# Deformable convolution and covariance attention on one core: square root as a recurrence on S = Z Y, and a shorter prologue

## The chip, the cores and the metric

One core of a Trainium2 chip. The time is the device time of one execution in microseconds, the median of several. The engines are called PE (matrix products), DVE (vector), ACT (activation), POOL (general), and SP (which here only issues transfers). All data are float32.

## The reference

The input x is 8 images of 64 channels, 24 x 24 pixels. Two residual blocks follow each other:

```
n  = groupnorm(x, 32 groups)
off = conv3x3(pad(n), w_off)                 # 128 output channels: y and x offsets of each of 64 channels
xd = bilinear sample of pad(n) at grid + off # per channel
x1 = x + w_pw @ relu(batchnorm(xd) * gamma + beta)

m  = groupnorm(x1, 32 groups)
A  = covariance of the 64 channels of m      # one 64 x 64 matrix per image
Y, Z = A / trace(A), I
for i in range(5):                           # Newton-Schulz iterations
    T = 0.5 * (3 I - Z @ Y)
    Y, Z = Y @ T, T @ Z                      # (Z is not needed after the last)
v  = mean over rows of Y * sqrt(trace(A))
a  = sigmoid(w2 @ relu(w1 @ v + b1) + b2)
out = x1 + a * m
```

## The kernel before

The work is written out by hand, one instruction stream per engine, with semaphores between them (a queue of an engine never reorders). Images are held in pairs, two images of 64 channels on 128 partitions, so there are four tiles of x (T = 4).

Prologue. SP issues the four tiles of x (lines 309 and 311), then waits until DVE has zeroed the buffer of w_pw (line 770) and issues six small transfers (lines 315 to 320); behind these in SP's queue stands, for each image from 1 on, the copy of its map shifted by a row (line 342), which the convolution of that image needs (line 584). ACT issues the two transfers of w_off. DVE first makes constants with 48 memsets, two 32x32 transposes and four comparisons for the identity (line 763; with it PE can start) and four operations for the matrix pairm that averages a pair of channels (line 767). Then come statistics of the first tile (line 799), a product with pairm on PE (line 562), a square root on ACT, and two ACT fills of the map of image 0, the second of them the copy shifted by a row (lines 430 and 432). PE meanwhile runs four fillers, products of the identity with itself whose result nobody reads (stay_busy, line 555), and turns w_off into nine taps by products with the identity (line 572, 24 instructions; a float32 product is two instructions), then eight fillers more (line 579). DVE copies four of six columns of taps from PSUM to SBUF (line 820) and ACT two (line 469). Then PE convolves the images in order: 12 instructions at line 588 with weights of row pairs, 12 at line 594 with those of the last row. In the convolution of image 0 the statistics product of the other three tiles stands between the two parts.

Middle. For each image ACT evicts the offsets and DVE does the sampling (lines 830 to 866). Then one far sample per partition is found, gathered, and put in its place; PE runs 26 and 15 fillers there (lines 621 and 625) ahead of and behind the batch norm products (lines 623 and 624). The pointwise products, group norm, transposes and covariances follow.

Recurrence. The four pairs are cut into halves of two (NS_HALF). DVE makes Y from the covariance (line 1061), Z = 1.5 I - 0.5 Y (line 1065) and 1.5 Y. PE forms Y Y; DVE turns that into the next Y (line 1074). Three times: PE forms Z Y (64 columns a product, line 695), DVE the factor T = 1.5 I - 0.5 Z Y, PE T [Y, Z] (128 columns), and DVE (line 1084, half 0) and ACT (line 534, half 1) copy 256 columns each back. One filler stands behind each group of products. At the end, row sums (line 1089), two rounds of matrix times vector (line 703) with DVE steps between give the vector of the last product; then scaling (line 1098), the two small layers (lines 738 and 741), and the result (lines 545 and 1109), which SP stores.

Of the kernel before, what the change touches and what calls it, by code (L numbers as in the profile page):

```python
# [5 lines left out]
def deform_conv_then_covariance_attention(nc, x, w_off, gamma, beta, w_pw, w1, b1, w2, b2, out):  # L6
# [17 lines left out]
    P = 128  # L24
# [30 lines left out]
    with ctx:  # L55
# [23 lines left out]
        lane = sb("lane", [P, 2, 32])  # L79
        lanet = sb("lane_of_partition", [P, 2, 32])  # L80
        halves = sb("one_half", [P, 32])
        pairm = sb("mean_of_group_pair", [P, P])
# [67 lines left out]
        u = sb("ns_col_sum", [P, T])  # L150
        zu = sb("ns_z_u", [P, T])
# [19 lines left out]
        P_BANK, YZ_BANK = (0, 3), (1, 2)  # L171
# [28 lines left out]
        gm_ok = sem("conv_map_ready")  # L200
        shifted_in = [sem(f"map_{b}_shifted_by_a_row_in") for b in range(B)]
# [48 lines left out]
        y_ok = sem("ns_y_ready")  # L250
        p_ps = sem("ns_product_in_psum")
        t_ok = sem("ns_t_ready")
        yz_ps = sem("ns_next_y_z_in_psum")
        yz_ok = [sem(f"ns_y_z_ready_{k}") for k in range(2)]
# [42 lines left out]

        def rows(ap):
            return ap.rearrange("p (r k) -> p r k", k=W)
# [112 lines left out]
        def _(act):  # L412
# [13 lines left out]
            def fill_gmap(b):  # L426
                if b == 0:
                    act.wait_ge(maps_zero, 5)
                full, gn = normalised(b)
                last = nc.scalar.activation(interior(b, 0, 2, 2), full, **gn)  # L430
                if b == 0:
                    last = nc.scalar.activation(interior(b, C, 1, 2), full, **gn)
                last.then_inc(gm_ok, 1)
# [34 lines left out]
            act.wait_ge(wtrans, 1)  # L468
            nc.scalar.copy(wt[:, 4:6, :].rearrange("p a n -> p (a n)"), ps[:, 6, 0:2 * P]).then_inc(wready, 1)
# [16 lines left out]
            act.wait_ge(wtrans, 2)  # L486
# [45 lines left out]
            for k in range(ITERS - 2):  # L532
                act.wait_ge(yz_ps, 2 * k + 2)
                nc.scalar.copy(YZ[:, T // 2:T].rearrange("p t m c -> p (t m c)"),
                               ps[:, YZ_BANK[1], 0:T * C]).then_inc(yz_ok[1], 1)
# [13 lines left out]
        def _(pe):  # L549
# [25 lines left out]
            for at, (first, second) in enumerate(((0, 3), (1, 4), (2, 5), (6, 6), (7, 7), (8, 8))):  # L575
                tap_to(lower, 5 + at // 4, at % 4, first)
                last = tap_to(upper, 5 + at // 4, at % 4, second)
            last.then_inc(wtrans, 1)
            stay_busy(8, 7)
            def conv(b, par, between=None):  # L580

                pe.wait_ge(gm_ok, b + 1)
                if between is None:
                    pe.wait_ge(shifted_in[b], 16)
                chunks = ((0, CA, F0, slice(0, C), 0), (CA, PAIRS, BANK, slice(C, P), GR))
# [4 lines left out]
                if between is not None:  # L590
                    between()
                for kx in range(3):
# [6 lines left out]
            pe.wait_ge(wready, 2)  # L599
# [19 lines left out]
            pe.wait_ge(wready, 3)  # L619
# [70 lines left out]
            def products(t0, t1, bank, left, right, width):  # L690

                for t in range(t0, t1):
                    for par in range(2):
                        h = slice(C * par, C * par + C)
                        last = mm(ps[h, bank, width * (t - t0):width * (t - t0 + 1)], left[h, t], right[h, t],  # L695
                                  start=True, stop=True)
                return last

            def vectors(col, left, right):
                for t in range(T):  # L700
                    for par in range(2):
                        h = slice(C * par, C * par + C)
                        last = mm(pstat[h, col + t:col + t + 1], left[h, t], right[h, t:t + 1], start=True, stop=True)
                last.then_inc(vec_ps, 1)

            Y, Z = YZ[:, :, 0], YZ[:, :, 1]
            both = YZ[:].rearrange("p t m c -> p t (m c)")

            def first_products(g):
                pe.wait_ge(y_ok, g + 1)  # L710
                products(*NS_HALF[g], P_BANK[g], Y, Y, C).then_inc(p_ps, 1)
# [8 lines left out]
            for g in range(2):  # L720
                first_products(g)
            stay_busy(1, 5)
            for k in range(ITERS - 2):

                for g, (t0, t1) in enumerate(NS_HALF):
                    pe.wait_ge(yz_ok[g], k + 1)
                    products(t0, t1, P_BANK[g], Z, Y, C).then_inc(p_ps, 1)
                stay_busy(1, 5)
                for g, (t0, t1) in enumerate(NS_HALF):
                    pe.wait_ge(t_ok, 2 * k + g + 1)  # L730
                    products(t0, t1, YZ_BANK[g], Tm, both, 2 * C).then_inc(yz_ps, 1)
                stay_busy(1, 5)
            pe.wait_ge(vec_ok, 1)
            vectors(216, Z, u)
            pe.wait_ge(vec_ok, 2)
            vectors(224, Y, zu)
            pe.wait_ge(vec_ok, 3)
# [7 lines left out]
        def _(dve):  # L745
# [3 lines left out]
            for j in range(32):  # L749
                v.memset(lane[:, 0, j:j + 1], float(j))  # L750
            for j in range(16):
                last = v.memset(lane[:, 1, 2 * j:2 * j + 2], float(j))
            then(last)
            v.memset(halves[:], 0.5)
            v.memset(ident[:], 0.0)
            then(v.memset(pairm[:], 0.0))
            wait()
            for k in range(2):
                last = v.transpose(lanet[:, k], lane[:, k])
            link(last)  # L760
            for q in range(0, P, 32):
                blk = slice(q, q + 32)
                last = v.tensor_tensor(ident[blk, blk], lane[blk, 0], lanet[blk, 0], ALU.is_equal)
            last.then_inc(consts, 1)
            for q in range(0, P, 32):
                blk = slice(q, q + 32)
                last = v.scalar_tensor_tensor(pairm[blk, blk], lane[blk, 1], lanet[blk, 1, 0:1], halves[blk],
                                              ALU.is_equal, ALU.mult)
            last.then_inc(mats, 1)
            v.memset(wpn[:], 0.0).then_inc(wpn_zero, 1)  # L770
            v.memset(eps[:], EPS)
            v.memset(vv[:], 0.0)
            v.memset(zero[:], 0.0)
            v.memset(neg1[:], -1.0).then_inc(image_done, 1)
            v.memset(ones[:], 1.0)

            def over(m, k):

                g = m[:].rearrange("p (g k) -> p g k", k=k)
                return [g[:, :, j:j + 1].broadcast_to([P, P // k, k]) for j in range(k)]  # L780

# [23 lines left out]
            def gn1_scale(g, t0, t1):  # L805
# [3 lines left out]
                link(v.tensor_tensor(dev, mv1[:, t0:t1, 0], view[:, :, 0], ALU.subtract))  # L809
                link(v.tensor_tensor(dev, dev, dev, ALU.mult))  # L810
                v.tensor_tensor(v1[:, t0:t1], dev, view[:, :, 1], ALU.add).then_inc(gn1_v, 1)
                dve.wait_ge(gn1_sd, g)
                link(v.reciprocal(r1[:, t0:t1], v1[:, t0:t1]))
                v.scalar_tensor_tensor(nb1[:, t0:t1], view[:, :, 0], -1.0, r1[:, t0:t1], ALU.mult,  # L814
# [322 lines left out]
```

## Time and profile before

| | us |
|---|---|
| median of 3 runs | 129.51 |
| lowest, highest | 128.79, 130.43 |
| profiled execution, its own time | 129.9 |
| its span, first to last instruction | 128.1 |
| PE busy | 96.7 |
| DVE busy | 94.7 |
| ACT busy | 58.5 |
| mean granted clock of PE | 0.893 |

1.8 us of the profiled execution lie outside its span. Busy time of an engine is the union of its instructions; a share of busy time mixes stages that have different limits. The granted clock is a share of 2.4 GHz; 0.50 is the lower level, 1.2 GHz.

### The profile page before, as it was taken

How to read it: one execution, taken by the hardware profiler on the slowest of the kernel's cores; microseconds unless marked ns; L12 is line 12 of the kernel's file. 1: busy time of each engine (PE TensorE's matmuls, PEld its weight loads, DVE VectorE, ACT ScalarE, POOL GpSimd, SP SyncE). 2: the span in 40 equal slices, each digit the busy share in tenths (PEclk: the TensorE clock that was granted, in tenths of full speed). 3: DMA queues.
4: the chain of work that ended last, by engine and by line, in shares of the span. 5: the costliest groups of instructions: out<-in, count | busy, mean ns of one | idle time of the engine just before them, and what ended most of it. 6: DMA issues, size and time to landing. Idle time of an engine off the chain costs nothing.

```text
span 128.1 us, 1828 instructions
## 1 busy us (share of the span) xinstructions
PE 96.7 (75%) x631; PEld 75.2 (59%) x631; DVE 94.7 (74%) x296; ACT 58.5 (46%) x92; POOL 9.8 (8%) x22
## 2 busy tenths in 40 slices
PE   0699999999999999944910029999999899994100
PEld 0599777666776667713600029998697897873100
DVE  7829175859999999999999999685779846333600
ACT  3059567669697794674049000029126270120600
POOL 7003500000000003200000601000000000000000
PEclk9999999999999999998685555999999999998555
DMA  4920718753885491794000040000000000000076
GB/s 112 303 55 0 153 37 232 185 145 77 249 231 143 135 255 31 148 276 128 0 3 0 0 125 0 0 8 0 0 0 0 0 0 5 0 5 0 0 192 177
DMA packets 6393, 10.92 MB, mean 85 GB/s; under 512 B 1648, under 2 KB 3440, under 8 KB 6384
## 3 DMA queue, kind: packets, MB, share of 16 engines
q1 hardware_dynamic: 5824, 8.93, 26.1%
q0 software_dynamic: 400, 1.58, 5.3%
q10 hardware_dynamic: 160, 0.30, 0.9%
q8 instruction: 5, 0.08, 0.3%
q14 instruction: 4, 0.03, 0.1%
HBM read 3.10 MB, written 5.14 MB: 64 GB/s over the span
## 4 chain that ended last, share of the span: by engine, by line
PE 64%; DVE 17%; ACT 6%; issue 3%; DMA 3%; POOL 1%; DVEq 0%; POOLq 0%
PE ps L588 18%; PE ps L555 14%; PE ps L594 11%; PE ps L667 4%; PE ps L695 4%; DMA slot_map<-gmap_scratch,gather_rows 3%; PE ps L630 3%; PE ps L572 2%; PE ps L653 2%; DVE result L931 2%; DVE rows_at_x L851 2%; ACT rows_at_x L445 1%; PE ps L638 1%; ACT positive_offsets L460 1%; DVE result L1109 1%
## 5 line engine op out<-in xcount | busy, mean ns | idle before, releaser
L555 PE MATMUL ps<-ident 128*128 128x128 f32 x134 | 22.1, 323 | 15.3 <-DMA slot_map<-gmap_scratch,gather_rows 11.6
L555 PEld LDWEIGHTS ps<-ident 128*128 128x128 f32 x134 | 19.8, 230 | 17.0 <-issue 12.9
L588 PE MATMUL ps<-gmap,w_off_taps 128*128 128x336 f32 (+1 forms) x96 | 27.7, 437 | 0.0
L588 PEld LDWEIGHTS ps<-gmap,w_off_taps 128*128 128x128 f32 x96 | 17.5, 188 | 10.0 <-issue 3.3
L594 PE MATMUL ps<-gmap,w_off_taps 64*128 64x288 f32 (+1 forms) x96 | 15.9, 443 | 0.0
L594 PEld LDWEIGHTS ps<-gmap,w_off_taps 64*128 64x128 f32 x96 | 11.0, 185 | 3.3 <-issue 2.7
L451 ACT COPY offsets<-ps 64x576 f32<-64x576 f32 x8 | 5.0, 629 | 9.3 <-PE ps L594 9.3
L851 DVE COPY_PREDICATED rows_at_x<-positive_offsets,x_differences 128x864 f32<-128x864 int32 x8 | 9.0, 1130 | 0.0
L613 PE MATMUL ps<-x_halves,ident 128*128 128x288 f32 x16 | 6.2, 542 | 3.6 <-DMA x_halves<-in_x_dram 3.6
L858 DVE TENSOR_TENSOR rows_at_x<-rows_at_x,offsets 128x864 f32<-128x864 f32 x8 | 8.4, 1054 | 0.0
L866 DVE TENSOR_TENSOR rows_at_x<-rows_at_x,hmap 128x864 f32<-128x864 f32 x8 | 8.4, 1053 | 0.0
L430 ACT ACTIVATE gmap<-x_pairs,gn_shift,gn_rstd 64x576 f32<-64x576 f32 x8 | 7.0, 876 | 1.0 <-DVE gn_shift L814 0.9
L445 ACT COPY rows_at_x<-x_differences 128x864 f32<-128x864 f32 x8 | 7.2, 904 | 0.0
L498 ACT ACTIVATE bn_scalars<-bn_scalars,eps 128x1 f32<-128x1 f32 x1 | 0.3, 295 | 14.5 <-DVE bn_scalars L982 14.5
L613 PEld LDWEIGHTS ps<-x_halves,ident 128*128 128x128 f32 x16 | 3.9, 258 | 5.0 <-DMA x_halves<-in_x_dram 3.8
L516 ACT COPY centered_t<-ps 96x384 f32<-96x384 f32 x8 | 3.6, 475 | 5.8 <-PE ps L653 5.8
L845 DVE TENSOR_TENSOR largest_abs_offset<-abs_offsets 128x288 f32<-128x288 f32 x8 | 3.6, 455 | 3.5 <-ACT rows_at_x L445 2.1
L460 ACT ACTIVATE positive_offsets<-offsets 128x576 f32<-128x576 f32 x8 | 5.9, 740 | 0.3
L667 PE MATMUL ps<-centered_t 96*128 96x128 f32 x48 | 5.8, 278 | 0.0
L463 ACT ACTIVATE abs_offsets<-offsets 128x576 f32<-128x576 f32 x8 | 5.8, 724 | 0.0
L667 PEld LDWEIGHTS ps<-centered_t 96*128 96x128 f32 x48 | 5.5, 192 | 0.0
L994 DVE BATCH_NORM_STATS2 gn_stats<-ps 128x6 f32<-128x288 f32 x8 | 3.6, 458 | 2.3 <-PE ps L630 2.2
(183 smaller groups left out, 149.1 us busy)
## 6 DMA issues: line engine op xcount, KB each, us to landing
offset_scratch<-offsets SPq DMA_DIRECT2D x8, 288.0 KB, 2.6
gmap_scratch<-gmap SPq DMA_DIRECT2D x8, 196.0 KB, 3.1
gmap<-gmap SPq DMA_DIRECT2D x7, 189.0 KB, 2.5
hmap<-gmap SPq DMA_DIRECT2D x12, 98.0 KB, 2.5
x_pairs<-in_x_dram SPq DMA_DIRECT2D x4, 288.0 KB, 4.9
x_halves<-in_x_dram POOLq DMA_DIRECT2D x2, 576.0 KB, 7.1
out_dram<-result SPq DMA_DIRECT2D x2, 360.0 KB, 4.2
out_dram<-result SPq DMA_DIRECT2D x2, 216.0 KB, 3.0
```

What stands on the lines that cost most here:

```text
L430: last = nc.scalar.activation(interior(b, 0, 2, 2), full, **gn)
L445: nc.scalar.copy(rows3(hrow[:, par]), windows(dx[:, par, 0:HH, 0:W], 3, MC - 1)).then_inc(left_ok, 1)
L460: nc.scalar.activation(pos[:, par], kq, ACT.Relu)
L463: nc.scalar.activation(ab[:, par], kq, ACT.Abs).then_inc(abs_ok, 1)
L555: mm(ps[:, bank, 0:P], ident[:], ident[:], start=True, stop=True)
L588: mm(psf[:, par, col:col + PC * (m1 - m0)], wt[:, kx, :], conv_window(gmap[:, b], kx + 2 + 2 * GR * m0, m1 - m0), start=(kx == 0), stop=False)
L594: last = mm(psf[:, par, col:col + PC * (m1 - m0)], wt[half, 3 + kx, :], conv_window(gmap[half, b], 2 * GR - shift + kx + 2 + 2 * GR * m0, ...
L613: mm(ps[:, X1_BANK[b], 0:Q], ident[:], xh[:, b, :], start=True, stop=False)
L667: last = mm(pcov[t // (T // 2)][:, t % (T // 2)], m, m, start=(k == 0 and hh == 0), stop=(k == 2 and hh == 1))
L851: v.copy_predicated(rows3(h), windows(rows(pos[:, par, 1, :]), 3, 0).bitcast(i32), right).then_inc(along, 1)
L858: v.tensor_tensor(h, h, windows(off[:, b, :, 1], 3, 0), ALU.mult).then_inc(along, 1)
L866: v.tensor_tensor(rows3(h), rows3(h), windows(hmap[:, b, 0:HH, 1:1 + W], 3, GR), ALU.add).then_inc(along, 1)
```

## The change

Prologue: half as many lane constants; pairm is made in one operation from the identity and holds sums (the half goes into the three operations that read the products). SP waits for the first tile of x before it issues the other three. DVE instead of ACT makes the shifted copy of image 0's map. The taps are held three to a bank and evicted in two parts: the row pairs by DVE, the last row by ACT, with semaphores of their own; the convolution of image 0 waits for the pairs, and for the last row only between its two parts. The eight fillers behind the taps are gone. The constants that nobody needs yet, the zeroing of w_pw's buffer among them, move behind DVE's copy of the taps.

Recurrence: with S = Z Y and T = 1.5 I - 0.5 S the next S is S T T, so Y and Z needn't be kept. X holds per pair a vector u and the factor T, 65 columns. Each of four turns: PE forms T [u, T] (line 695's successor, bank Q), DVE (half 0) and ACT (half 1) copy 130 columns back, PE forms S T T (bank S; in the first turn with the column S u beside it, which becomes the next u by a copy of DVE), DVE makes the next T out of it, and ACT copies the next S. At the end one round of T u, and the scaling reads its result from PSUM. No fillers stand in it.

```diff
-        YZ = sb("ns_y_z", [P, T, 2, C])
-        Y15 = sb("ns_y_1_5", [P, T, C])
-        Tm = sb("ns_t", [P, T, C])
+        S = sb("ns_s", [P, T, C])
+        X = sb("ns_u_and_factor", [P, T, 1 + C])
...
             sp.dma_start(xp_[:, 0, :], x_pair[:, 0, :]).then_inc(x_in[0], 16)
+            sp.wait_ge(x_in[0], 16)
             for t in range(1, T):
...
-                    last = nc.scalar.activation(interior(b, C, 1, 2), full, **gn)
...
-            nc.scalar.copy(wt[:, 4:6, :]..., ps[:, 6, 0:2 * P]).then_inc(wready, 1)
+            act.wait_ge(wtrans, 2)
+            nc.scalar.copy(wt[:, 3:6, :]..., ps[:, 6, 0:3 * P]).then_inc(singles_ok, 1)
...
+            for k in range(ITERS - 1):
+                act.wait_ge(q_ps, 2 * k + 2)
+                nc.scalar.copy(X[:, T // 2:T], a_level(1)).then_inc(q_ok[1], 1)
+                for g, (t0, t1) in enumerate(NS_HALF):
+                    if k < ITERS - 2:
+                        act.wait_ge(t_ok, 2 * k + g + 3)
+                        if k == 0:
+                            act.wait_ge(u_ok, g + 1)
+                        nc.scalar.copy(S[:, t0:t1], b_level(g)[:, :, 1:1 + C]).then_inc(s_ok, 1)
...
-            stay_busy(8, 7)
...
-                if between is None:
+                if b:
                     pe.wait_ge(shifted_in[b], 16)
+                else:
+                    pe.wait_ge(first_shift_ok, 1)
+                    pe.wait_ge(pairs_ok, 1)
...
+            for k in range(ITERS - 1):
+                for g in range(2):
+                    pe.wait_ge(t_ok, 2 * k + g + 1)
+                    if k == 1:
+                        pe.wait_ge(u_ok, g + 1)
+                    products(g, a_level(g), factor, with_u).then_inc(q_ps, 1)
+                for g in range(2):
+                    pe.wait_ge(q_ok[g], k + 1)
+                    if k:
+                        pe.wait_ge(s_ok, 2 * k + g - 1)
+                        products(g, b_level(g)[:, :, 1:1 + C], S, square).then_inc(s_ps, 1)
+                    else:
+                        products(g, b_level(g), S, with_u).then_inc(s_ps, 1)
...
+            v.tensor_tensor(pairm[:]..., *over(ident, 2), ALU.add).then_inc(mats, 1)
...
+            v.tensor_scalar(interior(0, C, 1, 2), xp_[0:C, 0, :]..., r1[0:C, 0:1],
+                            nb1[0:C, 0:1], ALU.mult, ALU.add).then_inc(first_shift_ok, 1)
             dve.wait_ge(wtrans, 1)
-            v.tensor_copy(wt[:, 0:4, :]..., ps[:, 5, 0:4 * P]).then_inc(wready, 1)
+            v.tensor_copy(wt[:, 0:3, :]..., ps[:, 5, 0:3 * P]).then_inc(pairs_ok, 1)
+            later_constants()
             gn1_mean_var(1, T)
...
+            for k in range(ITERS - 1):
+                t0, t1 = NS_HALF[0]
+                dve.wait_ge(q_ps, 2 * k + 1)
+                v.tensor_copy(X[:, t0:t1], a_level(0)).then_inc(q_ok[0], 1)
+                for g, (t0, t1) in enumerate(NS_HALF):
+                    dve.wait_ge(s_ps, 2 * k + g + 1)
+                    v.scalar_tensor_tensor(X[:, t0:t1, 1:1 + C], b_level(g)[:, :, 1:1 + C], -0.5,
+                                           windows(id15[:], t1 - t0, 0), ALU.mult, ALU.add).then_inc(t_ok, 1)
+                    if k == 0:
+                        v.tensor_copy(X[:, t0:t1, 0], b_level(g)[:, :, 0]).then_inc(u_ok, 1)
```

## Rows read from the trace of the kernel before

**Rows 1.** Chain of waits, in order of time (start us, us, what).
```profile
5.18 0.83 DVE gn_stats L799 x2
...
6.94 2.77 PE ps L572 x24
9.71 3.01 PE ps L555 x16
12.73 3.21 PE ps L588 x12
...
17.98 3.40 PE ps L588 x12
```

**Rows 2.** Timeline, 0 to 13 us (start us, us busy, engine, operation).
```profile
1.71 0.48 DVE L752 MEMSET lane<- 128x2 f32 x16
...
2.57 0.31 DVE L759 STREAM_TRANSPOSE lane_of_partition<-lane 128x32 f32<-128x32 f32 x2
...
3.73 2.08 PE L555 MATMUL ps<-ident 128*128 128x128 f32 x8 [3.73 <-DVE ident L763]
...
5.01 0.56 SPq L315 DMA_DIRECT2D w_pw_natural<-in_L_conv_w_pw_dram  x1
...
6.38 0.56 PE L562 MATMUL ps<-gn_mean_var,mean_of_group_pair 128*128 128x2 f32 x2 [0.58 <-DVE gn_mean_var L802]
...
7.99 0.60 SPq L320 DMA_DIRECT2D b_col<-in_L_conv_b_dram  x1
...
8.28 0.88 ACT L430 ACTIVATE gmap<-x_pairs,gn_shift,gn_rstd 64x576 f32<-64x576 f32 x1 [0.43 <-DVE gn_shift L814]
...
9.76 0.69 DVE L820 COPY w_off_taps<-ps 128x512 f32<-128x512 f32 x1 [1.52 <-PE ps L572]
```

**Rows 3.** Windows of line 555 alone: busy us (instructions), granted clock.
```profile
9.75:11.75 2.00, 2.00 (x10) 2.00 (x11) 1.00 0.01 0
...
76.50:79.50 3.00, 3.00 (x16) 3.00 (x15) 0.50 0.00 0
81.00:83.50 2.50, 2.50 (x25) 2.50 (x24) 1.00 0.00 0
```

**Rows 4.** Waits of DVE, 18 to 70 us (us, times, longest).
```profile
DVE largest_abs_offset L845 <- ACT rows_at_x L445: 2.1, 2, 1.9
```

**Rows 5.** Timeline, 82 to 84 us.
```profile
82.70 0.15 DVE L971 TENSOR_TENSOR bn_mean_var<-bn_mean_var,slot_value_over_n 128x1 f32<-128x1 f32 x1
...
83.83 0.28 PE L623 MATMUL ps<-bn_mean_var,mean_of_halves 128*128 128x2 f32 x2
```

**Rows 6.** Timeline, recurrence, 107 to 118 us.
```profile
106.83 0.45 PE L695 MATMUL ps<-ns_y_z 64*64 64x64 f32 x8 [0.30 <-DVE ns_y_z L1061]
...
107.27 0.49 DVE L1074 SCALAR_TENSOR_TENSOR ns_y_z<-ps,ns_y 128x128 f32<-128x128 f32 x2
...
107.63 0.68 PE L695 MATMUL ps<-ns_y_z 64*64 64x64 f32 x16
...
108.66 1.09 PE L695 MATMUL ps<-ns_y_z,ns_t 64*64 64x128 f32 x16
109.36 0.42 DVE L1084 COPY ns_y_z<-ps 128x256 f32<-128x256 f32 x1 [0.71 <-PE ps L695]
...
109.80 0.37 ACT L534 COPY ns_y_z<-ps 128x256 f32<-128x256 f32 x1 [4.29 <-PE ps L695]
...
117.90 0.20 PE L738 MATMUL ps<-pooled,w_t 128*8 128x8 f32 x2 [0.69 <-DVE pooled L1098]
```

**Rows 7.** Windows of all engines, the recurrence and its end.
```profile
106.20:114.70 8.50, 8.20 (x125) 6.55 (x125) 4.30 (x15) 0.74 (x2) 0.00 (x0) 1.00 0.01 2
114.70:117.90 3.20, 1.67 (x35) 1.31 (x35) 1.15 (x7) 0.37 (x1) 0.00 (x0) 0.96 0.00 0
```

**Rows 8.** Tile x_pairs: its four transfers, issue to landing.
```profile
DMA to landing us min/median/max: 3.2/4.9/5.5
```

**Rows 9.** Page, section 6: transfers of the shifted map.
```profile
gmap<-gmap SPq DMA_DIRECT2D x7, 189.0 KB, 2.5
```

More of the change, by code:

```diff
@@ L78, in deform_conv_then_covariance_attention @@
         ident = sb("ident", [P, P])
[L79 to L82, printed above, removed]
+        lane = sb("lane", [P, 32])
+        lanet = sb("lane_of_partition", [P, 32])
+        pairm = sb("sum_of_group_pair", [P, P])
         halfm = sb("mean_of_halves", [P, P])
@@ L249, in deform_conv_then_covariance_attention @@
         sn_ok = sem("sqrt_norm_ready")
[L250 to L254, printed above, removed]
+        t_ok = sem("ns_factor_ready")
+        q_ps = sem("ns_factor_squared_in_psum")
+        q_ok = [sem(f"ns_factor_squared_ready_{k}") for k in range(2)]
+        s_ps = sem("ns_next_s_in_psum")
+        s_ok = sem("ns_next_s_ready")
+        u_ok = sem("ns_first_vector_ready")
         vec_ps = sem("ns_vector_in_psum")
@@ L429, in fill_gmap @@
                 full, gn = normalised(b)
-                last = nc.scalar.activation(interior(b, 0, 2, 2), full, **gn)
-                if b == 0:
-                    last = nc.scalar.activation(interior(b, C, 1, 2), full, **gn)
-                last.then_inc(gm_ok, 1)
+                nc.scalar.activation(interior(b, 0, 2, 2), full, **gn).then_inc(gm_ok, 1)
             def fill_hmap(b):
@@ L688, in _, with products @@
             covariance(1)
-            def products(t0, t1, bank, left, right, width):
+            def products(g, out, left, right):
+                t0, t1 = NS_HALF[g]
                 for t in range(t0, t1):
@@ L694, in products @@
                         h = slice(C * par, C * par + C)
-                        last = mm(ps[h, bank, width * (t - t0):width * (t - t0 + 1)], left[h, t], right[h, t],
-                                  start=True, stop=True)
-                return last
[L699 to L711, printed above, removed]
+                        last = mm(out[h, t - t0], left[h, t], right[h, t], start=True, stop=True)
+                return last
+            factor, square, with_u = X[:, :, 1:1 + C], X[:, :, 1:1 + C], X[:]
             for b in range(G2, B):
@@ L719, in _ @@
             pe.wait_ge(x1_late, G2)
[L720 to L729, printed above, removed]
-                    pe.wait_ge(t_ok, 2 * k + g + 1)
-                    products(t0, t1, YZ_BANK[g], Tm, both, 2 * C).then_inc(yz_ps, 1)
-                stay_busy(1, 5)
+            for k in range(ITERS - 1):
+                for g in range(2):
+                    pe.wait_ge(t_ok, 2 * k + g + 1)
+                    if k == 1:
[8 more added lines that the diff above has]
+                        products(g, b_level(g), S, with_u).then_inc(s_ps, 1)
+            pe.wait_ge(t_ok, 2 * ITERS)
+            for t in range(T):
+                for par in range(2):
+                    h = slice(C * par, C * par + C)
+                    last = mm(pstat[h, 216 + t:217 + t], factor[h, t], X[h, t, 0:1], start=True, stop=True)
+            last.then_inc(vec_ps, 1)
             pe.wait_ge(vec_ok, 1)
[L734 to L737, printed above, removed]
             mm(pstat[0:HID, 256:256 + B], w1t[:], vv[:].rearrange("p a n -> p (a n)"), start=True,
@@ L780, in over @@
                 return [g[:, :, j:j + 1].broadcast_to([P, P // k, k]) for j in range(k)]
+            dve.wait_ge(consts, 1)
+            v.tensor_tensor(pairm[:].rearrange("p (g k) -> p g k", k=2), *over(ident, 2), ALU.add).then_inc(mats, 1)
             def late_constants():
@@ L1067, in _ @@
-                then(v.tensor_scalar(Y15[:, t0:t1], YZ[:, t0:t1, 0], 1.5, None, ALU.mult))
-            wait()
-            def of_product(out, half, plus):
-                t0, t1 = NS_HALF[half]
-                prod = ps[:, P_BANK[half], 0:(t1 - t0) * C].rearrange("p (t c) -> p t c", c=C)
-                return v.scalar_tensor_tensor(out, prod, -0.5, plus, ALU.mult, ALU.add)
-            for g, (t0, t1) in enumerate(NS_HALF):
-                dve.wait_ge(p_ps, g + 1)
-                of_product(YZ[:, t0:t1, 0], g, Y15[:, t0:t1]).then_inc(yz_ok[g], 1)
```

102 lines of the change are left out of this document (43 added, 59 removed).

## The prediction

> **What bounds the kernel now.** I read the chain of waits first, in order of time, because a share of busy time says nothing about which engine a stage waits for. At the start it runs from the constants and statistics on DVE through the taps on PE (6.94 us) and into the fillers of line 555, 3.01 us; only then, at 12.73, comes the convolution of image 0, and 5.25 us later that of image 1 [rows 1]. The timeline shows that the fillers alone hold it: DVE's copy of the taps ends at 10.45, the map of image 0 was filled before that, and PE still works on products nobody reads until 12.7 [rows 2]. The same table shows what else stands ahead: PE gets the identity at 3.73, runs four fillers until 5.81, and its statistics product at 6.38 [rows 2].
>
> What the fillers buy is the clock. In 9.75 to 11.75 us ten of their instructions took 2.00 us, 200 ns each; that is the pace of 76.5 to 79.5, 16 in 3.00 us at a granted clock of 0.50, not that of 81.0 to 83.5, 25 in 2.50 us at 1.00 [rows 3]. The column says 1.00 in the first of these stretches too, so there I believe the durations: PE was at the lower level, 1.2 GHz. The convolutions of images 0 and 1, 3.21 and 3.40 us for the same twelve instructions, ran at the same pace [rows 1], so the level had risen shortly before 12.7. PE had then been nearly gapless since 6.4.
>
> From there the convolutions follow each other on PE. DVE is a second bound of that stage: between 18 and 70 us it waited for ACT's differences twice, 2.1 us in all, 1.9 of it once [rows 4]. Its full stretch begins after the convolution of image 1, so what counts is when image 1's convolution starts, not image 0's. In the middle the statistics are ready at 82.85 and PE takes them up at 83.83, behind its fillers [rows 5]; this is unchanged, and shifts with the rest give or take half a microsecond.
>
> The recurrence is latency. One half's product takes 0.45 us, and DVE starts on it 0.44 after its first instruction; 16 instructions of 64 columns take 0.68, of 128 columns 1.09; DVE's two factors 0.49, the copies of 256 columns 0.42 on DVE and 0.37 on ACT [rows 6]. PE is busy 8.20 of 8.50 us there, at a granted clock of 1.00, and part of that is again fillers [rows 7].
>
> **Prologue, on the path.** Sixteen two-column memsets took 0.48 us, one of two transposes is 0.15, and the memsets of pairm's matrix and of the halves lie in the 0.38 between these rows, say 0.2 [rows 2]. The identity is ready 0.8 earlier, at 2.9, and the four fillers end at 5.0. The single operation for pairm lies beside them, at no cost. The first tile of x landed within 3.2 us of its issue even with three tiles behind it [rows 8], so before 4.4; alone it can't be later. Its statistics (0.83, and an aggregation of some 0.2) end at about 4.6 [rows 1]. So the four fillers decide: the statistics product moves from 6.38 to 5.0, and everything behind it by 1.35. ACT's fill of the map begins at 6.9 instead of 8.28 and ends at 7.8; the taps begin at 5.6 and end at 8.35 (2.77 us, [rows 1, 2]), if w_off is in. The shifted copy takes ACT no second 0.87; on DVE 576 columns of 64 partitions aren't in the trace. ACT's 0.88 is the upper end, and the lower is 0.4; I take 0.65, ready at 7.6. The copy of the pairs is three quarters of 0.69, so 0.55 [rows 2], done at 8.15; if the fill takes 0.88 it ends at 8.4, still level with PE. The convolution of image 0 can start at 8.35 instead of 12.56 or so: 4.2 us gross. ACT's copy of the last row's taps lies beside the first part of it, which takes 3.2 or more, at no cost. So do the statistics of the later tiles: issued at 4.1 to 5.6 and landing by 5.5 us later at the worst, they are in by 11.1; DVE is done with them at 11 to 13, and PE asks for them after the first part, at 11.6 at the full clock. That is a stall of up to 1 us in the worst case, and none if the convolution starts at the lower level.
>
> Two things take part of it back. First the clock: the level rose near 12 us. If it does so again, 3.5 us of the convolution pass at half pace, which costs 1.75, and image 0 ends at 17.98 - 4.2 + 1.75 = 15.5. If the 0.8 us earlier start of PE brings the rise forward as much, 15.1. If it rises by 8.4, 13.8.
>
> Second, SP. The zeroing of w_pw's buffer now stands behind the copy of the taps, at 8.3. The six transfers behind it took SP from 5.01 to 8.59, 3.6 us [rows 2]; moved, they hold SP until 11.9. Behind them stands the shifted map of image 1, which landed 2.5 us after its issue [rows 9]: 14.4, or 14.9 if the wait in the queue is counted. Before, SP was long free. So image 1 can't start before 14.4 to 14.9, however fast the clock. The two corrections don't add, the later one decides: 15.1 to 15.5, I take 15.2, against 17.98. The prologue is worth 2.8, with 2.0 (the level rises 1.6 later) and 3.5 (only the transfer decides) as the ends.
>
> The Trainium skill (TensorE: Matmul & The Clock Gate, "What's actually happening") says that the throttled state is the default and that sustained activity releases it, at an instant that varies between runs. No row here shows that variation; by it the cold part of image 0 could be anything from nothing to all of it.
>
> **Recurrence.** From the factor of half 1 (ready about 107.1) a turn of one half is: product 0.44 until its reader starts, copy of 130 columns (between the 0.25 of 128 columns and 0.42 of 256, so 0.27), a handoff of 0.04, product 0.44, next factor 0.26, handoff 0.04: 1.5 us [rows 6]. PE issues four half groups in a turn, 0.34 each by the 16-instruction row, 1.36 in all: just hidden. In the first turn DVE also copies u for both halves, a small operation of 0.15 each [rows 5], and half 1's factor queues behind the first of them: 0.3. ACT's copies of S stand behind its copy of half 1 in the queue and have most of a turn; I cost them at nothing, and up to 0.2 a turn if they delay that copy. Four turns and 0.3 end at 113.4; the last round of vectors is at most the 0.68 of 16 instructions, then two scalings of 0.17: PE's next product stands at 114.5, not at 117.90 [rows 6]. Gone are the row sums, one vector round and three small DVE steps. Gain 3.4; 3.6 if the last round is shorter, 2.6 if each of 16 handoffs costs 0.05 more.
>
> **Sum.** 129.9 - 2.8 - 3.4 = 123.7 for the profiled execution. The median is 0.4 below it, which would give 123.3; I forecast 123.5.
>
> **Rivals.** (a) The clock falls in the recurrence. The fillers that kept PE busy 96% are gone, and products of 65 columns in quarter arrays take their place. For: in 114.7 to 117.9, with PE busy 1.67 of 3.20 us, the clock ended below 1.00 [rows 7]. Against: the record of the new recurrence should still show PE busy nine tenths. At half pace a turn is bound by PE, 4 x 0.66 = 2.6 us instead of 1.5; two turns of it cost 2.2, four 4.4 (that would be more than the gain of the recurrence): 125.7 to 127.9, most likely the former.
> The Trainium skill (TensorE: Matmul & The Clock Gate, "A second HAM failure mode: psum-queue depth-cycling") speaks against this change in just this place: short idle pieces between groups of products can make the clock oscillate. By that rule the time would be that of (a); rows 7 show no such case while the fillers stand.
>
> (b) 65 columns with a stride of 65 cost like 128. Then a half group is 0.55, a turn is bound by PE at 2.2, 2.8 us more: 126.3. For: nothing but that the odd width isn't in the trace. Against: time there goes with the columns, 0.68 to 1.09.
>
> (c) The prologue gives nothing: the level rises so late that image 0 passes wholly at the lower level, 8.35 + 10.7 = 19.0. Then 129.9 + 1.0 - 3.4 = 127.5, inside 2%.
>
> (d) Slower: without fillers ahead and with a stop for the shifted map between, PE stays at the lower level through the convolutions of images 0 and 1. Each takes 5.3 more: 129.9 - 7.6 + 10.7 = 133.0. It comes out slower than before once the level rises later than 23.5 us (15.2 us at half pace eat 7.6). Against: PE is as busy from 8.35 on as it was when the level rose before.
>
> (e) It doesn't do what it says: the first tile alone delays the other three and PE stalls on them for a microsecond or two, 125.
>
> **Chances.** Forecast (122.3 to 124.6) 0.62; (a) 0.14, a third of it above 126.9; (b) 0.05; (c) 0.05; (d) 0.02; (e) 0.08; below 122.3, with a rise that comes early, 0.04. The range 122.2 to 126.3 leaves out some 0.15. A measurement of this kernel tells about 2% (126.9) from no change. Faster by more: 0.89; within: 0.09; slower: 0.02.
>
> **What the profile after would show.** PE's statistics product at 5.0, the first instruction of line 588's successor near 8.4 and at half pace until about 12; the six small transfers of SP from 8.3 to 11.9 and the shifted map behind them; image 1 at 15.2. If image 1 waits for its transfer, SP was the limit; if the first convolution ends later, the clock. In the recurrence turns of 1.5 us, DVE ready for half 0 each time before PE's group, and the granted clock at 1.00 up to the last vector round. The prediction is wrong if a turn is over 2 us, if the clock column falls before 114, or if the middle stage gives back what the start gains, for instance by its fillers meeting the other level.

## The result

| | before | changed |
|---|---|---|
| median, us | 129.15 (4 runs) | 124.59 (4 runs) |
| lowest, highest | 128.74, 130.43 | 123.63, 126.03 |
| profiled execution, its own time | 129.9 | 126.03 |
| its span | 128.1 | 123.2 |

The ratio of the times is 0.9615, 95% interval 0.956 to 0.967: 4% faster. The forecast of 123.5 lies 1.1 us below the median, which stands at the upper edge of the prediction's own 122.3 to 124.6. In this and the later ratios, executions over 1.5% above the fastest of their kernel are left out, the profiled one of the changed kernel among them. That one had 2.8 us outside its span where the three others had 1.9 to 2.1, so I compare spans: 128.1 to 123.2, 4.9 us less, where 6.2 had been forecast.

The chain of waits of the changed kernel, in order of time, with the lines that answer to [rows 1]:

```profile
0.74 3.31 DMA x_pairs<-in_x_dram
...
4.07 0.83 DVE gn_stats L800 x2
...
5.84 2.77 PE ps L585 x24
8.62 4.44 PE ps L604 x12
...
15.10 3.40 PE ps L604 x12
...
73.17 8.82 PE ps L568 x52
81.98 0.12 PE ps L639 x2
```

Taps go straight over into the convolution of image 0 (line 604), which starts 3.99 us earlier than before by the timeline (8.57 against 12.56). Its first twelve instructions take 4.44 us, where the same twelve of image 1 take 3.40 at the higher level, so some 1.0 us was lost to the lower level. Image 1 starts 2.88 us earlier. That difference stays through the convolutions and the sampling; then about 0.85 of it is gone. The timeline of that place, to be held beside [rows 5]:

```profile
73.17 8.82 PE L568 MATMUL ps<-ident 128*128 128x128 f32 x52 [10.58 <-DMA slot_map<-gmap_scratch,gather_rows]
...
79.83 0.15 DVE L977 TENSOR_TENSOR bn_mean_var<-bn_mean_var,slot_value_over_n 128x1 f32<-128x1 f32 x1
...
81.82 0.28 PE L639 MATMUL ps<-bn_mean_var,mean_of_halves 128*128 128x2 f32 x2
```

The statistics were ready at 79.98, 2.87 earlier than before; PE came to them at 81.82, only 2.01 earlier. The 26 fillers, unchanged in number, began 2.82 earlier (73.17 against 75.99) but took 8.82 us instead of 8.00. Windows of the fillers' line alone show why (PE's busy time and instructions, those of its weight loads, the granted clock, then two columns of the transfers):

```profile
73.50:78.50 5.00, 5.00 (x25) 5.00 (x25) 0.50 0.00 0
79.20:81.70 2.50, 2.50 (x24) 2.50 (x24) 1.00 0.00 0
```

Before, the level rose 4.1 us after the first of these fillers; here it rose 5.8 after it.

From there to the end the difference grows to 4.9 again. The timeline of the recurrence, for [rows 6] (L712 are its products, L1076 and L542 the copies, L1079 the next factor):

```profile
104.79 0.29 DVE L1070 SCALAR_TENSOR_TENSOR ns_u_and_factor<-ns_s,ident_times 128x128 f32<-128x128 f32 x1
...
108.15 0.91 PE L712 MATMUL ps<-ns_u_and_factor 64*64 64x65 f32 x16
108.26 0.29 DVE L1079 SCALAR_TENSOR_TENSOR ns_u_and_factor<-ps,ident_times 128x128 f32<-128x128 f32 x1 [0.17 <-PE ps L712]
...
108.64 0.29 DVE L1076 COPY ns_u_and_factor<-ps 128x130 f32<-128x130 f32 x1
108.99 0.74 PEld L712 LDWEIGHTS ps<-ns_u_and_factor,ns_s 64*64 64x64 f32 x16
108.99 0.88 PE L712 MATMUL ps<-ns_u_and_factor,ns_s 64*64 64x64 f32 x16
109.10 0.27 ACT L542 COPY ns_u_and_factor<-ps 128x130 f32<-128x130 f32 x1 [0.25 <-PE ps L712]
...
109.49 0.72 DVE L1079 SCALAR_TENSOR_TENSOR ns_u_and_factor<-ps,ident_times 128x128 f32<-128x128 f32 x2 [0.55 <-PE ps L712]
...
112.99 0.20 PE L744 MATMUL ps<-pooled,w_t 128*8 128x8 f32 x2 [0.43 <-DVE pooled L1088]
```

Read it as one turn of half 0: product at 108.15, DVE's copy of it at 108.64, product with S at 108.99, next factor at 109.49. From the first factor of half 1 to the first small layer it is 8.20 us, where it was 11.09.

In the kernel before, this stage was bound by PE, and its fillers were on the path. Its chain of waits has no gap between 106.83 and 114.71:

```profile
107.28 0.42 PE ps L555 x2
107.70 0.61 PE ps L695 x16
108.31 0.42 PE ps L555 x2
108.73 1.02 PE ps L695 x16
109.75 0.42 PE ps L555 x2
```

A turn there is 0.61 + 0.42 + 1.02 + 0.42 = 2.47 us of PE, and the seven fillers together are 2.9 us. How much of the gain is theirs, m_rec_fill shows below. The granted clock held in the new recurrence, by the windows of all engines there (for [rows 7]):

```profile
104.20:111.90 7.70, 6.53 (x128) 4.90 (x126) 4.48 (x17) 2.67 (x10) 0.00 (x0) 1.00 0.00 0
111.90:113.00 1.10, 0.64 (x17) 0.56 (x18) 0.32 (x2) 0.00 (x0) 0.00 (x0) 1.00 0.00 0
```

### The profile page after: what moved, and what is told of

The parts are those of the page before. It is cut to its first block, busy times and chain, and to the rows that moved or that the text cites. A ratio compares the mean times of both kernels' runs of the same rounds, so it can differ in the third digit from the quotient of the medians.

```text
span 123.2 us, 1759 instructions
## 1 busy us (share of the span) xinstructions
PE 93.8 (76%) x601; PEld 71.9 (58%) x601; DVE 92.9 (75%) x273; ACT 59.3 (48%) x98; POOL 9.9 (8%) x22
## 3 DMA queue, kind: packets, MB, share of 16 engines
HBM read 3.10 MB, written 5.14 MB: 67 GB/s over the span
## 4 chain that ended last, share of the span: by engine, by line
PE 64%; DVE 14%; DMA 6%; ACT 6%; issue 3%; POOL 1%; DVEq 0%; POOLq 0%
PE ps L604 20%; PE ps L568 11%; PE ps L611 11%; PE ps L712 5%; PE ps L683 5%; DMA slot_map<-gmap_scratch,gather_rows 3%; PE ps L646 3%; DMA x_pairs<-in_x_dram 3%; PE ps L585 2%; PE ps L669 2%; DVE result L937 2%; DVE rows_at_x L857 2%; ACT rows_at_x L453 1%; PE ps L654 1%; ACT positive_offsets L468 1%
## 5 line engine op out<-in xcount | busy, mean ns | idle before, releaser
L604 PE MATMUL ps<-gmap,w_off_taps 128*128 128x336 f32 (+1 forms) x96 | 28.8, 450 | 0.0
L568 PE MATMUL ps<-ident 128*128 128x128 f32 x104 | 16.4, 327 | 13.6 <-DMA slot_map<-gmap_scratch,gather_rows 10.6
L604 PEld LDWEIGHTS ps<-gmap,w_off_taps 128*128 128x128 f32 x96 | 18.1, 195 | 10.7 <-issue 4.3
L568 PEld LDWEIGHTS ps<-ident 128*128 128x128 f32 x104 | 15.7, 239 | 14.1 <-issue 11.0
L629 PE MATMUL ps<-x_halves,ident 128*128 128x288 f32 x16 | 7.0, 594 | 4.0 <-DMA x_halves<-in_x_dram 4.0
L501 ACT ACTIVATE relu_out<-largest_abs_offset,minus_one 128x2304 f32<-128x2304 f32 x1 | 2.2, 2215 | 6.6 <-DVE sampled L869 6.6
```

Of the source, the lines that this page charges most:

```text
L568: mm(ps[:, bank, 0:P], ident[:], ident[:], start=True, stop=True)
L604: mm(psf[:, par, col:col + PC * (m1 - m0)], wt[:, kx, :], conv_window(gmap[:, b], kx + 2 + 2 * GR * m0, m1 - m0), start=(kx == 0), stop=False)
L629: mm(ps[:, X1_BANK[b], 0:Q], ident[:], xh[:, b, :], start=True, stop=False)
```

## The experiments

All were timed in five rounds against the kernel before, those of a group on one chip. For each the median is given, and the ratio to the kernel before with its 95% interval.

**One half of the change each.** The hunks of the other half were left out.

```diff
 pro_only: no hunk of lines 144, 168, 247, 295, 529, 687, 717, 1058 (recurrence)
 rec_only: these hunks alone, and the memset of u
```

> The new prologue alone, the recurrence as before. Theory: the prologue takes 2.9 us off the start of the convolution of image 1 (17.9 to 15.0), and the middle gives part of it back where its 26 fillers run at the lower level for longer; so 126.0 to 127.0 against 129.2, with the recurrence as before: 11.1 us from the first factor of half 1 to the first small layer. Rival: the middle gives nothing back on the average, its 8.8 us in the changed kernel are chance; then 126.3 and fillers of 8.0 us or less. Rival: the two parts interact; then it is under 1 us faster or over 4.

> The new recurrence alone, the prologue as before. Theory: 2.9 us less from the last covariance to the first small layer, the granted clock at 1.00 until the last vector round, a turn of 1.66 us, made of products that their readers take up 0.49 to 0.50 us after their start; 126.3 against 129.2. Rival: the turn is bound by PE's issue of four groups; then the idle time of PE in a turn is nil and its groups follow each other at 0.34. Rival: the clock falls in it in some runs; then over 127.5 in those.

Measured: pro_only 127.53 us, 0.9884 (0.982 to 0.9948), against 129.59; rec_only 127.04, 0.9773 (0.969 to 0.9856). So the prologue alone gains less than 2%, and for the recurrence alone the interval has 2% inside it. The recurrence did what its theory says. From the first factor of half 1 to the small layer it took 8.19 us, as in the changed kernel, with its granted clock at 1.00 until after it:

```profile
107.11 0.29 DVE L1068 SCALAR_TENSOR_TENSOR ns_u_and_factor<-ns_s,ident_times 128x128 f32<-128x128 f32 x1
...
115.30 0.20 PE L741 MATMUL ps<-pooled,w_t 128*8 128x8 f32 x2 [0.44 <-DVE pooled L1086]
```

In time it gained 2.6 us by the medians and 2.9 by the ratio. The prologue gained only 1.5 to 2.1, and 127.53 lies outside the 126.0 to 127.0 of its theory. The profile of pro_only, of 127.03 us, the lowest of the six, has fillers of 7.84 us: nothing was given back in it. The two gains, 3.4% together, are near the 3.85% of the whole, so they don't interact by more than the intervals allow.

pro_only shows something more, in its timeline:

```profile
8.83 3.46 PE L591 MATMUL ps<-gmap,w_off_taps 128*128 128x336 f32 x12
...
10.66 0.87 ACT L433 ACTIVATE gmap<-x_pairs,gn_shift,gn_rstd 64x576 f32<-64x576 f32 x1
...
11.85 0.60 SPq L323 DMA_DIRECT2D b_col<-in_L_conv_b_dram  x1
12.48 0.60 SPq L345 DMA_DIRECT2D gmap<-gmap  x1
...
15.23 1.10 PE L591 MATMUL ps<-gmap,w_off_taps 128*128 128x336 f32 x3 [0.90 <-ACT gmap L433]
```

Here the first convolution ran at the full clock, 3.46 us; it was over at 14.3, and PE idled 0.90 us. The releaser named, ACT's fill of the map, had ended at 11.53; what came last is the transfer, which SP issued at 12.48 behind its small ones and which landed 2.6 us later, at 15.1. So the two limits of the prediction both exist, and lie within 0.2 us of each other: image 1 starts at 15.03 when the clock costs some 1.0, and at 15.23 when it costs nothing. In m_rec_fill, further down, with the same prologue, the transfer is named as the releaser outright:

```profile
15.29 3.44 PE L604 MATMUL ps<-gmap,w_off_taps 128*128 128x336 f32 x12 [0.16 <-DMA gmap<-gmap]
```

**Fewer fillers in the middle of the changed kernel.**

```diff
-            stay_busy(26, 7)
+            stay_busy(16, 7)
```

> The changed kernel with 16 instead of 26 fillers ahead of the batch norm products. Theory: PE ran fillers until 81.8 in the changed kernel where the statistics were ready at 80.0, so the fillers set the end of this stage; with ten fewer (2.3 us at the higher level, 4.5 at the lower) the products start when the statistics are ready: 1.0 to 1.9 us faster. Rival: with fewer fillers the clock is still at the lower level when the second batch of fillers and the pointwise products start, and the time comes back there: no change or 1 us slower.

> The kernel with 16 fillers in the middle once more, as the base of the three that run beside it. Theory: the spread of the changed kernel (123.6 to 126.0) was that of its 26 fillers, which take longer or shorter by when PE's level rises in them; with 16 the statistics are the later ones, so the times lie within 0.4 us of each other again, at 123.3. Rival: the narrow spread was chance, and they lie 1 us or more apart.

Measured: 123.31 us, 0.9537 (0.9478 to 0.9596), lowest to highest 123.06 to 123.41; once more, on another chip: 123.20, 0.9489 (0.9444 to 0.9534), 122.94 to 123.61. It is 1.3 to 1.4 us faster than the changed kernel's 124.59, and its twelve times lie within 0.7 us where four of that one spread over 2.4. PE was waiting for the statistics, not they for PE, though the level rose as late as 6 us after the first filler:

```profile
73.31 6.70 PE L568 MATMUL ps<-ident 128*128 128x128 f32 x32 [10.55 <-DMA slot_map<-gmap_scratch,gather_rows]
...
80.01 0.15 DVE L977 TENSOR_TENSOR bn_mean_var<-bn_mean_var,slot_value_over_n 128x1 f32<-128x1 f32 x1
...
80.22 0.38 PE L639 MATMUL ps<-bn_mean_var,mean_of_halves 128*128 128x2 f32 x2 [0.21 <-DVE bn_mean_var L977]
```

**The same in the kernel before**, one edit, to measure the change with the fillers out of the way.

> The kernel before with 16 instead of 26 fillers in the middle, its prologue and recurrence untouched. Theory: its statistics were ready at 82.85 and PE came to them at 83.83, so it wins 1.0 us at most in a run like the profiled one: 128.4. Against it the changed kernel with 16 fillers (123.2) is then 5.2 us faster or more, near the 2.9 of the prologue and 2.9 of the recurrence that the traces show, where the two kernels as they are differ by 4.6: the difference was given back in the fillers. Rival: 129.6, no gain; then the fillers gave nothing back on the average, and the prologue is worth less than its 2.9.

Measured: 128.88 us, 0.9961 (0.9933 to 0.9989): a gain of 0.5, half of what the one profile had promised. The difference to the changed kernel with 16 fillers is 5.6 to 5.7 us by the medians (128.88 less 123.31 or 123.20), against 4.6 to 5.0 with 26 in both. That is what the traces give stage by stage, 2.9 and 2.9, within 0.2. So by the times 0.6 to 1.1 us of the change's gain was given back in the fillers. The intervals are as wide as that, so the times only agree with the 0.85 of the profile; they don't show it by themselves. In its profile another part varies: the eight fillers behind the taps, which the change drops, took 2.15 us and not 3.08 as in the kernel before, and image 1 started at 16.98, not 17.91. Against such a run the prologue is worth 1.9 and not 2.9, which may be why pro_only came out at the lower end.

**Only four fillers in the middle.**

```diff
-            stay_busy(26, 7)
+            stay_busy(4, 7)
```

> The changed kernel with 4 fillers in the middle instead of 26. Theory: what the fillers buy is the clock; with four PE idles some 5 us ahead of the statistics, the level is the lower one there, and the 15 fillers and the pointwise products behind them run in part at half pace: 1.5 to 3 us slower than with 16, some 125 to 126. Rival: the fillers buy nothing; then it is as fast as with 16, 123.2.

Measured: 125.59 us, 0.9705 (0.9657 to 0.9753), 2.3 us slower than with 16. Its profile is of its highest time, 126.96: there the first tile landed at 4.41, image 0's first part took 4.96 us, and image 1 started at 15.84, 0.6 later than in mid16. The rest is lost here: the 15 fillers that follow the batch norm products take 6.15 us instead of 3.60, at a granted clock of 0.50 until 87. Windows of all engines of mid16 and then of mid4, 80 to 88 us:

```profile
80.00:88.00 8.00, 7.79 (x52) 6.70 (x51) 6.58 (x19) 3.72 (x6) 0.00 (x0) 1.00 0.00 1
```

```profile
80.00:88.00 8.00, 7.13 (x36) 7.08 (x37) 4.51 (x13) 3.44 (x5) 0.00 (x0) 0.55 0.00 0
```

So the fillers do earn the clock, and 16 of the 26 were enough for it; between 4 and 16 nothing was run.

**Fillers behind the taps put back** in the changed kernel, and, with 16 in the middle, **the first four fillers dropped**.

```diff
+            stay_busy(8, 7)              # fill8, behind the taps
-            stay_busy(4, 7)              # m_no_first4
```

> The changed kernel with the eight fillers behind the taps put back. Theory: they delay the first convolution by 8 x 0.43 = 3.4 us at the lower level, and give half of the time back that image 0 would have run at the lower level (1.2 us of loss in the changed kernel): 1.7 to 2.3 us slower than the changed kernel. Rival: they are worth what they cost, within 0.5 us, because image 1 waits for SP's queue anyway.

> 16 fillers in the middle, and without the first four fillers of PE. Theory: they end at 5.1, just before the statistics product can start at 5.3, so they cost 0.1 us at most; without them the level rises later and image 0 passes wholly or almost wholly at half pace, up to 5 us more, of which the wait for the map of image 1 hides none: 0.5 to 3 us slower. Rival: the level depends on the taps and what follows alone; no change, 123.2.

Measured: fill8 125.07 us, 0.9655 (0.9586 to 0.9724), 0.5 above the changed kernel with overlapping intervals; m_no_first4 123.26, 0.9539 (0.95 to 0.9578), no change. Both theories of mine missed, and both measured times are those of the rivals. In fill8 the reason is not the rival's, though: the eight took 2.81 us, and image 0 then ran at the full clock, 11.11 to 16.45; image 1 began 1.4 us later than in the changed kernel, where I had 1.7 to 2.3 for the whole, and its middle fillers took 7.81 us, 1.0 less. In m_no_first4 the statistics product came at 4.93 instead of 5.35, mostly because the first tile landed 0.4 us sooner (its statistics began at 3.72 and not at 4.14); the four fillers, which end at 5.1 in the other profiles, would have hidden up to half of that. The taps and image 0 came 0.4 earlier with it. The first part of image 0 took 4.80 us, 1.35 more than the 3.45 of mid16_again, and image 1 began at 14.99, where it was 15.02. With the four fillers in place that first part took from 3.45 to 4.96 us in the profiles here, so 4.80 doesn't show that they bear on the level at all.

**Without SP's wait for the first tile**, on the kernel with 16.

```diff
-            sp.wait_ge(x_in[0], 16)
```

> That kernel without SP's wait for the first tile of x: all four tiles are issued at once. Theory: the first tile lands as before, some 3.3 us after its issue, since before it did so in 3.2 with three behind it; the wait's worth lies in w_off, which then shares the engines with three more tiles and lands at up to 6.4 instead of before 5.8; taps start up to 0.6 later, and image 0 too; image 1, which SP's queue holds at about 15, moves by less: 0 to 0.4 us slower. Rival: the wait does speed up the first tile; then the statistics start 0.5 us later or more.

Measured: 123.70 us, 0.9537 (0.949 to 0.9583), against 123.20 of mid16_again: 0.5 slower, with intervals that overlap. In the trace the first tile landed 3.0 us after its issue; with the wait it took 3.0 to 3.7 in ten profiles, so the wait does not bring it in sooner. The later of the two halves of w_off took 5.1 instead of 3.7, and PE had to wait for it:

```profile
5.00 0.56 PE L574 MATMUL ps<-gn_mean_var,sum_of_group_pair 128*128 128x2 f32 x2
...
6.42 2.84 PE L584 MATMUL ps<-ident,w_off_natural 128*64 128x128 f32 x24 [0.86 <-DMA w_off_natural<-in_L_conv_w_off_dram]
```

The taps start at 6.42, with the wait at 5.84. Image 1 moves by 0.15, and this execution took 123.23 us, no more than with the wait: what the medians differ by is not in this profile.

**w_pw's buffer zeroed early**, on the kernel with 16, so that SP's small transfers go out from 5.5 on.

```diff
+            v.memset(wpn[:], 0.0).then_inc(wpn_zero, 1)    # behind pairm
             def later_constants():
-                v.memset(wpn[:], 0.0).then_inc(wpn_zero, 1)
```

> That kernel with w_pw's buffer zeroed before the statistics of the first tile instead of behind the copy of the taps, so that SP issues its six small transfers some 3 us earlier and is free when the map of image 1 is ready at 11.3. Theory: the shifted map lands near 14 instead of 14.8 to 15.2; where the first convolution runs at the full clock from the start, image 1 starts up to 0.9 us earlier; where it loses 1.2 us to the lower level, nothing changes: 0 to 0.9 us faster, by the run. Rival: the zeroing and six transfers delay the first tile's statistics or w_off by as much.

Measured: 122.86 us, 0.9469 (0.9414 to 0.9523), 0.3 below mid16_again, not separated by the intervals. In its profile the shifted map was issued at 11.36 instead of 12.29 and image 1 started at 14.47, directly behind image 0, instead of 15.02 after an idle 0.90. The first tile's statistics were not delayed. Its six times spread over 1.7 us, though it too has 16 fillers in the middle. In the two runs with SP's queue as in the change, mid16 and mid16_again, image 0's first part took 4.66 and 3.45 us, and image 1 still started within 0.2 us, at 15.22 and 15.02. That SP's queue hid the level's varying rise there, and no longer does here, fits these rows; it is not shown by a run of its own.

**Fillers back in the recurrence**, on the kernel with 16.

```diff
+                stay_busy(1, 5)          # behind the two T [u, T]
+                stay_busy(1, 5)          # behind the two S T T
```

> That kernel with a filler of PE (0.21 us at the full clock) behind each pair of product groups of the recurrence, as there was before, eight in all. Theory: the turn is latency, PE idles 0.08 of the 0.42 us between groups, 0.34 a turn, so 0.42 of fillers a turn costs 0.1 to 0.25: 0.4 to 1.0 us slower in all, and the clock was never in play. Rival: PE is the bound of the turn; then each turn is longer by all of 0.42: 1.7 us slower. Rival: the fillers earn their place by the clock: not slower.

Measured: 124.61 us, 0.9604 (0.9557 to 0.9651), 1.4 slower than mid16_again. The price of a filler in my text was wrong: it is 0.42 us on the path, not 0.21, as in the chain of the kernel before. So 0.84 was added to each turn. The turn grew from 1.66 or 1.68 (by the half) to 2.06, from its timeline:

```profile
107.58 0.68 PE L712 MATMUL ps<-ns_u_and_factor 64*64 64x65 f32 x16
108.07 0.29 DVE L1078 COPY ns_u_and_factor<-ps 128x130 f32<-128x130 f32 x1 [0.51 <-PE ps L712]
108.19 0.49 PE L568 MATMUL ps<-ident 128*128 128x128 f32 x2
...
109.64 0.68 PE L712 MATMUL ps<-ns_u_and_factor 64*64 64x65 f32 x16
```

With fillers PE is the bound: two groups in 0.61 and a filler in 0.42, twice, is 2.06. Without them its own groups need 1.22 of 1.66 us, so the turn is latency, and of 0.84 of added work 0.44 went into the gaps. The clock stayed at 1.00 either way.

This run also divides the gain of the recurrence. From the first factor of half 1 (103.34) to the first small layer (112.81) it took 9.47 us, against 11.09 before, with fillers in both (eight here, seven there). So of the 2.9 us some 1.6 are the new recurrence itself, and 1.3 are fillers that it does without. One rival was not run: the old recurrence without its fillers. An estimate from [rows 6]: one half's turn there would be 0.49 until DVE takes up the product, 0.26 for the factor, 0.70 until the wide product is taken up, 0.42 for the copy and two handoffs of 0.04, 1.95 us in place of 2.47, or 1.6 us over three turns, by deleting the fillers alone.

**A faster version**: 16 fillers, w_pw early, and 11 instead of 15 behind the batch norm products.

```diff
-            stay_busy(15, 7)
+            stay_busy(11, 7)
```

> 16 fillers in the middle, w_pw's buffer zeroed early, and 11 instead of 15 fillers behind the batch norm products. Theory: with 15, PE leaves these fillers at 84.1, then spends 0.5 us on a product of x, and takes up ACT's first output, ready at 83.85, at 84.6; with four fewer (0.9 us at the full clock) it takes it up at 83.9: 0.7 us faster, 122.1 to 122.3. Rival: something else is late there (the second half of the sampled values), and nothing changes: 122.9.

Measured: 122.62 us, 0.9471 (0.9418 to 0.9524), three times at 121.8 to 122.1 and three at 123.2. The stage did shrink: from the batch norm product to the first pointwise product it is 84.38 - 80.62 = 3.76 us, where mid16 had 84.60 - 80.22 = 4.38, and PE now waits there for ACT's first output. In its profile image 0's first part took 4.95 us, 1.5 lost to the clock, and image 1 began at 15.60. What of the 0.6 arrives in the median can't be told from that spread; 15.60 against 14.47 of m_small_early is larger. It is the fastest median of all, 5.3% below the kernel before, and not separated from m_small_early.

## Why the prediction was right, and where it was off

- *The prologue, 2.8 us.* Image 1 started at 15.03, forecast 15.2: right, and for the reasons given. The fillers of line 555 held the convolution, image 0 could start at 8.57 (forecast 8.35), some 1.0 us went to the lower level (forecast 1.4 to 1.75), and SP's queue holds image 1 until 15.1 when the clock doesn't: pro_only and m_rec_fill show the wait itself, m_small_early its removal.
- *"The four fillers decide" when the statistics product starts.* Wrong by 0.3 us. The first tile landed at 4.07, so the statistics ended at 5.14 and not at 4.6; the product came at 5.28. I had taken the landing for no constraint. Dropping these fillers changed nothing in time.
- *The first tile alone "can't be later".* It was, 3.3 instead of 3.2 us, and up to 3.7 in other profiles; the wait's use is w_off, which came 1.4 sooner (m_no_x_wait). I had named no price for that.
- *DVE's shifted copy* took 0.57 (forecast 0.65, between 0.88 and a 0.4 for which no row stood), the copy of the pairs 0.56 (0.55), pairm and the copies beside other work nothing.
- *"The recurrence is latency".* Of the kernel before that was misread. PE was its bound: 7.87 of 7.90 us busy from 106.80 to 114.70, with the seven fillers, 2.9 us, on its path. The sum did not suffer, since it priced the new turns directly and took the old end from the trace. But by m_rec_fill some 1.3 us of the gain came from having no fillers there, and only 1.6 from the new recurrence.
- *The recurrence, 3.4 us.* It was 2.9. That the new turn is latency stands; the term that was too small is the turn, 1.5 us forecast and 1.66 measured. The step that failed is the reading "DVE starts on it 0.44 after its first instruction" in [rows 6]: DVE's operation at 107.27 was on half 0, whose product had been finished long before, and it only queued on DVE. The pair that belongs together is 107.63 and 108.12, 0.49. Twice a turn 0.05, and 0.29 instead of 0.26 for the factor, make 0.13; the remaining 0.03 are in the handoffs. The u copies cost 0.15 in the second turn, not 0.3 in the first.
- *Rival (a), the clock in the recurrence.* Out in every profile here: the column read 1.00 until the last vector round was over, though in mid16_again it fell 0.2 us behind it, and in the changed kernel between 113 and 114, behind the first small layer. The rule of the Trainium skill that I had weighed (TensorE: Matmul & The Clock Gate, "A second HAM failure mode: psum-queue depth-cycling") had no case, with gaps of some 0.11 us between groups (0.44 a turn over four of them).
- *Rival (b), 65 columns like 128.* Out: a product of 64x65 is taken up 0.49 us after its start, as one of 64x64.
- *Rivals (c) and (d), the level.* Out: no profile shows image 0 wholly at the lower level. The prediction let its cold part be "anything from nothing to all of it"; over the profiles with the new prologue and nothing behind the taps its first part took 3.45 to 4.96 us, a loss of nothing to 1.5.
- *Rival (e), the other three tiles.* Out: their statistics began at 8.66, behind DVE's constants, and were done at 11.24, while PE asked for them at 13.06.
- *The middle, "give or take half a microsecond".* This is the largest miss: 0.85 in the profile, and 0.6 to 1.1 by the times. I had named it as what would make the prediction wrong, and left it out of the sum though [rows 3] had both prices: a filler at the lower level costs twice, and PE came to the statistics only when its block of 26 was done, so the block's length decides. It was 7.8 to 8.8 us over the five profiles that have it, by when the level rose. Where in that range the changed kernel would fall, no row could have said; that most of a microsecond was at stake, the two prices say.

So 2.9 + 2.9 - 0.85 = 4.9 in the profile, against 2.8 + 3.4 = 6.2 forecast: the prologue 0.1 better, the recurrence 0.5 and the middle 0.85 worse. Not settled: why pro_only's median gained less than rec_only's by more than the profile of either shows. The phase of the clock in the kernel before (its image 1 started at 16.98, 17.91 and 18.11 in three profiles) can account for a microsecond, but no run fixes that phase.

## What to carry to other kernels

A block of fillers is priced at both levels of the clock, and sized so that at the lower level it ends when the work it waits for is ready; beyond that it is work on the path. Before an algorithm is credited with a stage's gain, delete the fillers from the old one: here they were 2.9 us of PE's path, and nearly half of the gain was theirs. When a chain of small steps is costed, take each latency from a pair in which the reader was idle and waiting, never from one that queued behind its own engine. When a transfer or a memset moves, follow the queue that it unblocks: here one zeroed buffer held the map of image 1 for most of a microsecond (11.36 against 12.29).

## What the runs showed of the hardware

- PE's level rose between 2.8 and 6.1 us after the first of the middle fillers, in the 13 profiles that have 16 or more of them; a block of 26 took 7.8 to 8.8 us. The Trainium skill (TensorE: Matmul & The Clock Gate, "What's actually happening") says that the instant varies from run to run; these profiles agree. mid16 and mid16_again are the same kernel: the level rose 6.1 us after the first of these fillers in the one and 3.8 in the other, and image 0's first part took 4.66 and 3.45 us.
- The granted clock's column can read 1.00 where the pace is that of 0.50. mid16's 32 filler instructions in the middle took 6.70 us, 209 ns each, 6.1 us of them at 0.50, and its next 30 took 3.60 at 1.00, 120 ns each. rec_only's 16 behind the taps took 3.28 us, 205 ns each, under a column of 1.00, and before_mid16's took 2.15 under the same.
- Three tiles queued behind the first on SP's queue did not delay it (3.0 us, against 3.0 to 3.7 when it went alone), but in that profile the later of the two transfers that ACT had issued beside it took 5.1 us, against 3.7 in mid16_again.
- A filler of two instructions cost 0.42 us on PE's path when it stood alone between groups of small products at a granted clock of 1.00 (m_rec_fill and the kernel before); in a block of 15 at the same clock 30 instructions took 3.59 us, 0.24 a filler.
